# Interleaving the two heads of a pair, token by token, in the query and key buffers of a local attention

## Chip, cores and metric

One Trainium2 chip, one core. The metric is the time of one launch on the device, in microseconds (us), as the median of several runs.

## What is computed

The input x has 2 x 2048 tokens of 256 channels, in f32. First an attention block, then a routed feed-forward block, each with a residual and a normalisation:

```python
qkv = x @ W_attn + b_attn                       # 16 heads of 16 channels
scores = einsum('bhtd,bhsd->bhts', q, k) / 4
scores = where((j <= i) & (j >= i - 64), scores, -inf)
out = softmax(scores) @ v
x = layernorm(x + out @ W_proj + b_proj)
expert_idx = argmax(x @ Wr.T)                   # 8 experts
inter = gelu(x @ W1[expert_idx] + b1[expert_idx])
x = layernorm(layernorm_affine(inter @ Wo + bo + x) + x)
```

## The kernel before, in words

**Order.** The program has a queue for each engine: SP (DMA issues), GpSimd (POOL), ScalarE (ACT), VectorE (DVE) and TensorE (PE), synchronised by semaphores written out by hand. Each runs the loop `for it in range(FIRST, LAST + 1)` over 32 tiles of 128 tokens (`it` from -4 to 31) in software-pipelined order. PE in step `it` does, in this order: `scores(0)`, the output projection of tile it-2, the transposes of x for tile it+4 (line 1641), `scores(1)`, `values(0)`, `scores(2)`, `scores(3)`, `values(1)`, the value projection of tile it+1, the transposes of tile it's maxima (line 1683), the query and key projection of tile it+4 (`queries_keys`, lines 1599 to 1619), and `scores_t(0)` to `scores_t(3)` with the transposes of the attention of tile it-1 between them. Steps -4 to -1 are setup and fill the pipeline. After step 31 the routed feed-forward (`walk_slots`) runs 36 tiles over slots sorted by expert.

**Precision.** Operands in f16 are split into a high and a low part; a product is three matmuls (`product`, line 1428).

**Queries and keys.** `queries_keys` writes 4 groups of 128 output channels (2 for queries, 2 for keys; the index m % 2 is the half: heads 0 to 7 or 8 to 15) for 128 tokens into one PSUM bank, each by 7 matmuls: 2 x 3 of `product` and one for the bias (line 1617). The view of the bank is `ps_qk` (line 259): [query or key, half, token]. ACT copies it to f16 (`qk_hi`, line 955), DVE makes the low part (line 1326). Both wait in the steps' order: ACT after the maxima rows, then come its exps; DVE's low part is the last of its step but for small things. When two tiles are there, SP stores a tile pair to the DRAM tensor `qk_s` by six stores (`store_part`, line 401), then loads it turned, by head: the 16 channels of a head times three terms (high, high, low and their partners) become 48 partitions.

**Loads.** `stacks_begin` (line 476), on SP in even steps, waits for the stores and for the last scores of two pairs before (the buffers `qs` and `ks` are double), and loads the queries (line 483) and the key window of half 0; `stacks_end` (line 487), one step later, loads the window of half 1 and the keys of the second block. A block is 64 queries; its window holds 128 keys and begins 64 tokens earlier, so `windows` (line 467) takes two loads for each half: the new tokens (line 471, runs of 384 bytes) and the last 64 of the pair before (line 474, runs of 128 bytes). PE waits for queries and half 0 at step 0 of a tile's scores, for half 1 (`chunk_ld`) at step 1, for the second block (`second_ld`) at step 2.

**Scores.** They are computed twice. `scores(step)` (line 1560): queries stationary (112 x 64), keys moving (112 x 128), the two heads of a strip side by side in the array's two column halves, 8 matmuls a step, 4 steps a tile. VectorE takes maxima over keys (line 1227). The maxima of all heads are turned by PE (line 1683) into PSUM rows and copied by ScalarE (`maxima_rows`, line 882, two calls a tile, 32 x 1024 elements) into the partitions of `qs` above 96, so that `scores_t(step)` (line 1588: keys stationary, 128 x 128, queries moving, 128 x 64, again 4 x 8) gives scores with the maximum taken off and the mask added; ScalarE's exps (line 879) read them. Mask rows stand in the odd partitions of `ks` (constants), unit rows in those of `qs`; partitions above 96 of `ks` hold window rows that pick a head's maximum. All of these are built at the start by POOL (lines 615 to 693) in a staging area (`mask_w`, `ident_w`, `last_rows`), copied by DVE (line 1013), a DMA (`constant_rows`, line 442), ACT (line 961) and POOL (lines 669, 691).

In memory `qs` is [partition, head, 256 tokens] and `ks` [partition, block, head, 256 tokens], the head index being 2 x pair + half. A matmul's operand takes one head:

```python
def queries(t, c, i, e, b):
    return qs[t // 2 % 2][:, CC * (2 * i + e) + c, t % 2 * P + b * BLK:t % 2 * P + b * BLK + BLK]
def keys(t, c, i, e, b):
    return ks[t // 2 % 2][:, b, CC * (2 * i + e) + c, t % 2 * P:t % 2 * P + P]
```

## Time and profile before

| | us |
|---|---|
| median of 3 runs | 523.68 |
| their range | 520.51 to 526.76 |
| the profiled execution's own time | 522.61 |
| its span, first to last instruction | 520.9 |
| granted TensorE clock over the span | 0.981 of full |

The profile is of one execution. Its times are in us unless marked ns; L1560 is line 1560 of the kernel. PE is TensorE's matmuls, PEld its weight loads, which overlap them; matmuls overlap each other, so that their start distances tell the pace and not their durations. In a row of the timeline stand the start, the time from the first start to the last end, engine, line, operation, output and inputs with shapes, and the count of instructions merged. "[0.75 <-X]" is idle time before it and what ended it; "issue" is idle time in which the profile shows nothing waited for.

### The profile page before, as it was taken

How to read it: one execution, taken by the hardware profiler on the slowest of the kernel's cores; microseconds unless marked ns; L12 is line 12 of the kernel's file. 1: busy time of each engine (PE TensorE's matmuls, PEld its weight loads, DVE VectorE, ACT ScalarE, POOL GpSimd, SP SyncE). 2: the span in 40 equal slices, each digit the busy share in tenths (PEclk: the TensorE clock that was granted, in tenths of full speed). 3: DMA queues.
4: the chain of work that ended last, by engine and by line, in shares of the span. 5: the costliest groups of instructions: out<-in, count | busy, mean ns of one | idle time of the engine just before them, and what ended most of it. 6: DMA issues, size and time to landing. Idle time of an engine off the chain costs nothing. (4 is left out here: it accounts for less than half of the span.)

```text
span 520.9 us, 24517 instructions
## 1 busy us (share of the span) xinstructions
PE 482.8 (93%) x8591; PEld 433.4 (83%) x8591; DVE 423.2 (81%) x1115; ACT 349.6 (67%) x793; POOL 365.3 (70%) x638
## 2 busy tenths in 40 slices
PE   8999998999999989989989899999999999999980
PEld 5678987988988978988877698888999999999970
DVE  6568687789888896877889558799999998998892
ACT  3567585867778785858676686666666666677740
POOL 7983566565757664747566656888888887888884
PEclk9999899999999998989999999999999999999996
DMA  8796486588785777676664122222333366246200
GB/s 225 201 239 168 136 214 170 151 210 215 198 218 167 226 195 191 187 205 182 177 170 99 44 63 64 62 74 74 111 97 84 93 223 243 78 144 222 69 18 14
DMA packets 83000, 77.08 MB, mean 148 GB/s; under 512 B 31046, under 2 KB 74639, under 8 KB 82834
## 3 DMA queue, kind: packets, MB, share of 16 engines
q1 hardware_dynamic: 79250, 66.80, 46.9%
q0 software_dynamic: 3248, 8.41, 4.6%
q8 instruction: 73, 1.20, 1.0%
q14 instruction: 45, 0.37, 0.2%
q10 hardware_dynamic: 384, 0.30, 0.2%
HBM read 43.48 MB, written 23.55 MB: 129 GB/s over the span
## 5 line engine op out<-in xcount | busy, mean ns | idle before, releaser
L1793 PE MATMUL ps<-wo_hi,ks 128*128 128x256 f16 x576 | 128.5, 273 | 5.2 <-DVE ks L1349 5.2
L1811 PE MATMUL ps<-sT_lo,w_hi 128*128 128x128 f16 x496 | 104.3, 219 | 0.0
L1811 PE MATMUL ps<-sT_hi,w_lo 128*128 128x128 f16 x496 | 104.3, 219 | 0.0
L1811 PE MATMUL ps<-sT_hi,w_hi 128*128 128x128 f16 x496 | 104.2, 219 | 0.0
L1227 DVE TENSOR_REDUCE mx<-ps 128x4 bf16<-128x512 f32 x128 | 83.7, 674 | 6.6 <-PE ps L1560 6.3
L736 POOL DMA_INDIRECT slots<-row,slot_of x32 | 33.9, 1059 | 68.3 <-PE ps L1560 39.9
L1793 PE MATMUL ps<-wo_lo,ks 128*128 128x256 f16 x288 | 78.5, 273 | 0.0
L1454 PE MATMUL ps<-v_even,probs 128*64 128x17 f32 x1024 | 68.0, 208 | 2.2 <-issue 1.5
L1454 PE MATMUL ps<-v_odd,probs 128*64 128x17 f32 x1024 | 68.2, 208 | 1.5 <-issue 1.5
L1454 PEld LDWEIGHTS ps<-v_odd,probs 128*64 128x64 f32 x1024 | 64.9, 138 | 3.1 <-issue 3.1
L879 ACT ACTIVATE probs<-ps 128x512 f32<-128x512 f32 x128 | 66.0, 611 | 0.1
L1454 PEld LDWEIGHTS ps<-v_even,probs 128*64 128x64 f32 x1024 | 64.8, 138 | 0.9 <-ACT probs L879 0.8
L885 ACT ACTIVATE qs<-ps 32x1024 f16<-32x1024 bf16 x64 | 61.3, 1004 | 6.0 <-PE ps L1683 5.3
L991 ACT ACTIVATE g_even<-ps,b1T 128x128 f32<-128x128 f32 (+1 forms) x168 | 44.2, 353 | 28.9 <-PE ps L1811 28.5
L1793 PEld LDWEIGHTS ps<-wo_hi,ks 128*128 128x128 f16 x576 | 53.0, 98 | 9.0 <-DVE ks L1349 6.4
L991 ACT ACTIVATE probs<-ps,b1T 128x128 f32<-128x128 f32 x144 | 41.0, 367 | 28.3 <-PE ps L1811 27.7
L941 ACT ACTIVATE v_odd<-ps 128x256 f32<-128x256 f32 x32 | 12.3, 383 | 67.8 <-PE ps L1432 67.8
L1432 PE MATMUL ps<-xT_hi,wa_lo 128*128 128x128 f16 x256 | 52.1, 227 | 0.8 <-issue 0.8
L1432 PE MATMUL ps<-xT_lo,wa_hi 128*128 128x128 f16 x256 | 52.2, 227 | 0.1
L1811 PEld LDWEIGHTS ps<-sT_hi,w_lo 128*128 x496 | 48.5, 98 | 4.4
L1432 PE MATMUL ps<-xT_hi,wa_hi 128*128 128x128 f16 x256 | 52.0, 227 | 0.0
L1588 PE MATMUL ps<-qs,ks 128*128 128x64 f16 x1024 | 48.6, 194 | 3.3 <-DVE attT L1307 1.1
(276 smaller groups left out, 1570.3 us busy)
## 6 DMA issues: line engine op xcount, KB each, us to landing
qk_s<-qk_hi SPq DMA_DIRECT2D x64, 128.0 KB
w_in<-in_L_ffn_W_dram SPq DMA_DIRECT2D x30, 256.0 KB, 2.9
qs<-qk_s SPq DMA_DIRECT2D x16, 384.0 KB, 4.3
ks<-qk_s SPq DMA_DIRECT2D x16, 384.0 KB, 5.4
ks<-qk_s SPq DMA_DIRECT2D x32, 144.0 KB, 4.1
v_odd<-slots SPq DMA_DIRECT2D x32, 128.5 KB
qk_s<-qk_lo SPq DMA_DIRECT2D x30, 128.0 KB
v_odd<-slots SPq DMA_DIRECT2D x30, 128.0 KB
```

The costliest lines, as they stand in the source:

```text
L736: nc.gpsimd.indirect_dma_start(out=slots, out_offset=bass.IndirectOffsetOnAxis(ap=slot_of[n // 2 % 2][:, n % 2:n % 2 + 1], axis=0), in_=ro ...
L879: nc.scalar.activation(probs[:, u, :, :, :], ps_t[step].rearrange("p (i e q) -> p i e q", i=STRIPS, e=2), ACT.Exp, scale=SCALE).then_inc(e ...
L885: nc.scalar.activation(q.rearrange("p (i h) n -> p i h n", i=STRIPS), ps_mx[0:P - ALIGNED].rearrange("p e m n -> p (e m) n").unsqueeze(1) ...
L941: nc.scalar.activation(v_odd[m % VRING][:, :, 0:HD], ps_v[:, 0:C].rearrange("p (h d) -> p h d", d=HD), ACT.Copy)\
L991: last = nc.scalar.activation(g[1 - p][:, ic, n * width:(n + 1) * width], (ps_h_first[half] if j < 0 else ps_h[1 - p][:, half, :])[:, col ...
L1227: nc.vector.tensor_reduce(mx[it % 2][:, at:at + STRIPS], ps_s[step].rearrange("p (i k) -> p i k", k=P), AX.X, ALU.max)\
L1432: last = mm(dst, l, r, start=start and n == 0, stop=stop and n == len(terms) - 1)
L1454: last = mm(ps_num[BLK * b:BLK * b + BLK, head, :], probs[:, 2 * c + b, i, e, :], v[:, head, :], start=True, stop=True, tile_position=(0, ...
L1588: last = mm(ps_t[step][:, at:at + BLK], keys(it, c, i, e, b), queries(it, c, i, e, b), start=i + e == 0 and not first, stop=i + e == STRIP ...
L1793: ins = mm(ps_y[p], h[p][hs][:, ic, :], wo[ws][:, ic, :], start=n == 0, stop=n == 3 * IC - 1)
L1811: up_ins = mm(ps_h[1 - p][:, half, col + m * width:col + (m + 1) * width], weights(ws, owners[m], k, ic), sT[1 - p][ss][:, k, at], start=k ...
```

## The change

The two halves become the innermost index of everything that holds queries and keys. `ps_qk` is read as [query or key, token, half]: a projection matmul writes 128 f32 results at a step of two elements. `qk_hi`, `qk_lo`, `qs`, `ks` and the staging area have the half last; `queries` and `keys` give operands whose elements step by two f16. `qk_s` becomes [query or key, channel, term, token, half] over all tokens, so that the window of a tile pair is one run across the pair boundary: `stacks_begin` issues two loads (queries; the whole key window of both halves), `stacks_end` one (keys of the second block). `chunk_ld` goes. `maxima_rows` issues one instruction for each half, 32 x 512 elements, which writes at a step of two; there are four a tile in place of two. The staging area's mask and unit rows are twice as wide (512 elements), so the memsets and selects that build them are; the copies of them keep their element counts. No other arithmetic changes. The core of the diff:

```diff
-    qk_s = nc.dram_tensor("qk_s", [2, TILES // 2, P, 3, CC, 2 * P], f16, kind="Internal").ap()
+    qk_s = nc.dram_tensor("qk_s", [2, P, 3, N, CC], f16, kind="Internal").ap()
-        qk = [[sb(f"qk{k}_{s}", [P, 2, CC, 2 * P], f16) for s in ("hi", "lo")] for k in range(2)]
+        qk = [[sb(f"qk{k}_{s}", [P, 2, 2 * P, CC], f16) for s in ("hi", "lo")] for k in range(2)]
-        qs = [sb(f"qs{k}", [P, HEADS, 2 * P], f16) for k in range(2)]
-        ks = [sb(f"ks{k}", [P, 2, HEADS, 2 * P], f16) for k in range(2)]
+        qs = [sb(f"qs{k}", [P, PAIRS, 2 * P, CC], f16) for k in range(2)]
+        ks = [sb(f"ks{k}", [P, 2, PAIRS, 2 * P, CC], f16) for k in range(2)]
-        mask_w = stage[:, 0:2 * P]
-        ident_w = stage[:, 2 * P:4 * P]
+        mask_w = stage[:, 0:CC * 2 * P]
+        ident_w = stage[:, CC * 2 * P:CC * 4 * P]
...
         def ps_qk(t):
-            return ps[:, 6 if t < LEAD and t % 2 else 0, :].rearrange("p (w m t) -> p w m t", w=2, m=CC)
+            return ps[:, 6 if t < LEAD and t % 2 else 0, :].rearrange("p (w n m) -> p w n m", w=2, m=CC)
...
-            eng.dma_start(qk_s[w, g, :, term, :, :].rearrange("p m n -> p (m n)"),
-                          qk[g % 2][PARTS[w][term]][:, w, :, :].rearrange("p m n -> p (m n)")).then_inc(qk_st[g % 2], 16)
+            eng.dma_start(qk_s[w, :, term, 2 * P * g:2 * P * (g + 1), :].rearrange("p n m -> p (n m)"),
+                          qk[g % 2][PARTS[w][term]][:, w, :, :].rearrange("p n m -> p (n m)")).then_inc(qk_st[g % 2], 16)
...
-            def windows(g, m, new, landing):
-
-                k = g % 2
-                dst = ks[k][0:ALIGNED:2, 0, :, :].rearrange("r (h m) n -> r h m n", m=CC)[:, :, m, :]
-                sp.dma_start(dst[:, :, BLK:2 * P], new[:, :, m, 0:2 * P - BLK]).then_inc(landing, 16)
-                if g > 0:
-                    prev = qk_s[1, g - 1].rearrange("(h d) j m n -> (d j) h m n", d=HD)
-                    sp.dma_start(dst[:, :, 0:BLK], prev[:, :, m, 2 * P - BLK:2 * P]).then_inc(landing, 16)
+            def stack_rows(w, first, last):
+
+                return qk_s[w, :, :, first:last, :].rearrange("(h d) j n m -> (d j) h (n m)", d=HD)
...
-                windows(g, 0, new, stack_ld[k])
+                sp.dma_start(qs[k][0:ALIGNED:2, :, :, :].rearrange("r h n m -> r h (n m)"),
+                             stack_rows(0, 2 * P * g, 2 * P * (g + 1))).then_inc(stack_ld[k], 16)
+                behind = BLK if g > 0 else 0
+                sp.dma_start(ks[k][0:ALIGNED:2, 0, :, BLK - behind:2 * P, :].rearrange("r h n m -> r h (n m)"),
+                             stack_rows(1, 2 * P * g - behind, 2 * P * (g + 1) - BLK)).then_inc(stack_ld[k], 16)
...
-                windows(g, 1, new, chunk_ld[k])
...
-                    nc.scalar.activation(q.rearrange("p (i h) n -> p i h n", i=STRIPS),
-                                         ps_mx[0:P - ALIGNED].rearrange("p e m n -> p (e m) n").unsqueeze(1)
-                                         .broadcast_to([P - ALIGNED, STRIPS, 2 * CC, BLK]),
-                                         ACT.Copy, scale=1.0 / ONE).then_inc(mxT_out, 1)
+                    for m in range(CC):
+                        last = nc.scalar.activation(
+                            q[:, :, :, m].rearrange("p (i e) n -> p i e n", i=STRIPS),
+                            ps_mx[0:P - ALIGNED, :, m, :].unsqueeze(1).broadcast_to([P - ALIGNED, STRIPS, 2, BLK]),
+                            ACT.Copy, scale=1.0 / ONE)
+                    last.then_inc(mxT_out, 1)
...
             def queries(t, c, i, e, b):
-                return qs[t // 2 % 2][:, CC * (2 * i + e) + c, t % 2 * P + b * BLK:t % 2 * P + b * BLK + BLK]
+                return qs[t // 2 % 2][:, 2 * i + e, t % 2 * P + b * BLK:t % 2 * P + b * BLK + BLK, c]
...
-                return ks[t // 2 % 2][:, b, CC * (2 * i + e) + c, t % 2 * P:t % 2 * P + P]
+                return ks[t // 2 % 2][:, b, 2 * i + e, t % 2 * P:t % 2 * P + P, c]
...
-                        pe.wait_ge(stack_ld[pair % 2], 16 * (pair // 2 + 1 + window_loads(pair)))
+                        pe.wait_ge(stack_ld[pair % 2], 16 * 2 * (pair // 2 + 1))
                         wait(pe, mxT_out, 2 * it)
-                    if step == 1:
-                        pe.wait_ge(chunk_ld[pair % 2], 16 * window_loads(pair))
...
-                        dst = ps_qk(new)[:, m // CC, m % CC, :]
+                        dst = ps_qk(new)[:, m // CC, :, m % CC]
```

## Rows read from the trace of the kernel before

**Rows 1.** The page, part 1: busy us (share of the span) and instructions.

```profile
PE 482.8 (93%) x8591; PEld 433.4 (83%) x8591; DVE 423.2 (81%) x1115; ACT 349.6 (67%) x793; POOL 365.3 (70%) x638
```

**Rows 2.** Stretches, us: PE, PEld, DVE, ACT, POOL busy (count), PEclk, DMA share, GB/s.

```profile
24.00:300.00 276.00, 259.41 (x5561) 230.06 (x5558) 221.94 (x605) 195.68 (x348) 170.84 (x352) 0.98 0.67 180
...
300.00:521.00 221.00, 202.40 (x2852) 189.20 (x2849) 187.11 (x484) 142.26 (x423) 174.22 (x232) 0.98 0.32 102
...
120.00:160.00 40.00, 39.48 (x881) 35.90 (x877) 35.20 (x99) 31.13 (x57) 26.12 (x55) 1.00 0.78 206
```

**Rows 3.** The maxima's transposes (line 1683): all, then two of the timeline.

```profile
L1683 PE MATMUL ps<-ident_b,mx x64: 217/219/314, 28.0 to 295.5; 128*128 128x128 bf16 x64
...
90.18 0.28 PE L1683 MATMUL ps<-ident_b,mx 128*128 128x128 bf16 x2
...
98.04 0.28 PE L1683 MATMUL ps<-ident_b,mx 128*128 128x128 bf16 x2
```

**Rows 4.** Waits: who waited for whom; us in total, times, longest.

```profile
PE ps L1432 <- issue: 3.1, 2, 2.3
...
PE ps L1454 <- issue: 3.0, 2, 1.5
...
PE ps L1560 <- DMA ks<-qk_s: 2.6, 2, 1.7
...
PEld ps L1588 <- ACT qs L885: 4.5, 16, 0.9
```

**Rows 5.** Timeline of PE in a tile, then durations of three lines.

```profile
90.29 0.22 PE L1432 MATMUL ps<-xT_hi,wa_hi 128*128 128x128 f16 x1
...
90.40 0.22 PE L1432 MATMUL ps<-xT_lo,wa_hi 128*128 128x128 f16 x1
...
156.83 0.40 PE L1588 MATMUL ps<-qs,ks 128*128 128x64 f16 x8
...
158.78 0.41 PE L1560 MATMUL ps<-ks,qs 112*64 112x128 f16 x8
...
159.82 0.38 PE L1641 MATMUL ps<-ident,xin 128*128 128x128 f32 x2
...
L1588 PE MATMUL ps<-qs,ks 128*128 128x64 f16 x1024 | 48.6, 194 | 3.3 <-DVE attT L1307 1.1
...
L1560 PE MATMUL ps<-ks,qs 112*64 112x128 f16 x1024 | 46.4, 222 | 3.5 <-DMA ks<-qk_s 2.6 <-DVE mx L1227 0.7
...
L1641 PE MATMUL ps<-ident,xin x46: 272/273/474, 3.0 to 256.0; 128*128 128x128 f32 x46
```

**Rows 6.** Timeline of ScalarE (ACT) in one tile: maxima copies, exps.

```profile
155.46 1.92 ACT L885 ACTIVATE qs<-ps 32x1024 f16<-32x1024 bf16 x2
...
157.90 2.06 ACT L879 ACTIVATE probs<-ps 128x512 f32<-128x512 f32 x4
```

**Rows 7.** Timeline of the setup: POOL, and the first scores of PE.

```profile
1.63 0.51 POOL L619 MEMSET bqk<- 128x512 f16 x1
...
2.20 0.31 POOL L625 MEMSET probs<- 128x256 f16 x1
...
2.66 0.42 POOL L626 TENSOR_SCALAR_AFFINE_SELECT probs<-probs 96x256 f16<-96x256 f16 x1
...
4.15 2.54 POOL L634 TENSOR_SCALAR_AFFINE_SELECT probs<-probs 128x256 f16<-128x256 f16 x2
...
23.33 0.10 POOL L685 MEMSET eps_ffn<- 128x1 f32 x1
...
23.53 0.37 PE L1555 MATMUL ps<-shut,ones_b 1*128 1x512 bf16 x1 [0.75 <-DMA ks<-qk_s]
```

**Rows 8.** DMA: packets of the page, then issues (count, KB, us to landing).

```profile
DMA packets 83000, 77.08 MB, mean 148 GB/s; under 512 B 31046, under 2 KB 74639, under 8 KB 82834
...
ks<-qk_s SPq DMA_DIRECT2D x32, 144.0 KB, 4.1
...
ks<-qk_s SPq DMA_DIRECT2D x30, 48.0 KB, 4.7
```

More of the change, by code:

```diff
@@ L235, in attention_then_routed_ffn @@
         w1_mixed = [[[spare[4 * b + 2 * m + s] for s in range(2)] for m in range(PARTS_M)] for b in range(2)]
[L236 removed]
+        h = [[ks[k][:, :, :, :, :].rearrange("p b h n m -> p (b h n m)")[:, s * IC * P:(s + 1) * IC * P]
               .rearrange("p (i t) -> p i t", i=IC) for s in range(2)] for k in range(2)]
[L238 removed]
+        room = [qs[k][:, :, :, :].rearrange("p h n m -> p (h n m)").bitcast(f32) for k in range(2)]
         xbo, xbe, fin = ([room[k][:, n * C:(n + 1) * C] for k in range(2)] for n in range(3))
@@ L295, in attention_then_routed_ffn @@
         stack_ld = [sem(f"stack_ld{k}") for k in range(2)]
-        chunk_ld = [sem(f"chunk_ld{k}") for k in range(2)]
         second_ld = [sem(f"second_ld{k}") for k in range(2)]
@@ L361, in unit @@
             return step % CC, step // CC, 2 * (step % CC) + step // CC
-        def window_loads(g):
-            return sum(1 + (n > 0) for n in range(g % 2, g + 1, 2))
         def turned(it):
```

68 lines of the change are left out of this document (33 added, 35 removed).

## The prediction

> **What bounds the kernel now.** Read the engines' busy shares first [rows 1]: TensorE (PE) is busy for 93% of the span. The stretches [rows 2] split the span: the change touches what runs to about 300 us (setup and attention); the routed FFN behind it, 221 us, keeps its instructions. In the attention stretch PE is busy for 259.4 of 276 us. The transposes of the maxima come once per tile, the first at 28.0 and the last at 295.5 us [rows 3]: 31 steps, so 8.63 us per tile. The same rows show two of them 7.86 us apart (90.18 and 98.04); seven tiles of 7.86 to 7.90 us stand in this trace. 7.86 us is therefore what PE's own queue needs for a tile, and 0.77 us is the mean of what comes on top. The waits [rows 4] say what that is: 6.1 us in four long gaps put down to "issue", 2.6 us for the stack loads, and the weight load ahead of the second scores waits 4.5 us in 16 tiles for ScalarE's maxima rows. So the loads that the change merges cost PE 2.6 us in this stretch (and 0.75 us ahead of its first scores [rows 7]), while whatever adds PE time adds to nearly every tile.
>
> The spacing of matmuls is read from their starts, not from their durations, since they overlap [rows 5]: projections of 128 columns start at 90.29 and 90.40 with one between them, 55 to 56 ns apart; eight scores of the second kind (64 columns) take 0.40 us with one of 0.19 in it, so 0.21 / 7 = 30 ns apart; eight of the first kind (128 columns, in pairs for the two halves of the array) take 0.41 with 0.22 in it, 27 ns apart or 54 per pair; two transposes of 128 columns in f32 take 0.38 with 0.27 in it, 109 ns apart. TensorE's granted clock is 1.00 in such a stretch [rows 2], its level of 2.4 GHz.
>
> **The change part by part.**
>
> Projection of queries and keys. Per tile 4 x 7 = 28 matmuls now write every second f32 word of their PSUM bank. No row of before has such an output. From below it costs nothing (56 ns apart, as now). From above, take the nearest slower stream of the same 128 columns, the f32 transposes at 109 ns: +53 ns x 28 = 1.48 us per tile. I take the upper end. The reason from rows: 56 ns for 128 columns is 2.3 columns per ns, each 4 bytes on the way out, and no row of [rows 5] writes faster than that per column of the array, so the output side shows nothing to spare; two neighbouring results now lie 8 bytes apart, so if they were written together before, they can't be now. Of the 1.48 us, some 0.2 us fall into what now is waiting (ScalarE's maxima rows, below, end before the longer projection does), leaving 1.28. 28 projections run inside the attention tiles: 28 x 1.28 = 35.8 us. The four of the setup stand on a longer list of waits; I count 2 to 3 us for them.
>
> The Trainium skill bears on this where no row does: "PSUM — Partial Sum Buffer", Specifications, gives 8-byte lines and says that any non-contiguous access pattern slows matmuls significantly. By it the upper end would hold, by the rows alone either could. No run here shows it yet.
>
> Score operands. 32 matmuls of each kind per tile read both operands at a step of two f16. From below nothing; from above, again the f32 row, whose 128 columns bring 4 bytes each past the same port: the first kind 54 to 109 per pair, 16 x 55 = 0.88 us, the second kind 30 to 55, 32 x 25 = 0.80 us, together 1.7 us per tile. I take the lower end: the second kind loads 128 stationary columns within 30 ns [rows 5], 4.3 columns per ns, nearly twice what any moving stream uses, so the reading side shows room that the writing side doesn't.
>
> On this the Trainium skill ("SBUF — State Buffer", in the part on the DMA port swizzle) says that lines are 16 bytes and two hits in one are enough. Four f16 at step two share a line, so by it the scores would keep their pace; no row here tests it.
>
> ScalarE's maxima rows. Two instructions of 1024 elements become four of 512. The two take 1.92 us now, and the four exps, each of 512 elements out of PSUM, take 2.06 [rows 6]: four copies cost about what four exps do, +0.14 us per tile. Behind them on ScalarE wait the high part of queries and keys and the four exps, and behind these VectorE's low part and its maxima. If all of it showed, 32 x 0.14 = 4.5 us; half of the tiles have the weight load waiting there [rows 4], so 2 us. Under the longer projection it is nothing: the copies end 2.06 + 0.3 us after the maxima's transposes, the projection after 28 x 109 ns = 3.05 us.
>
> Setup on GpSimd (POOL). The two memsets and four selects that build the mask and the unit rows double in width. A memset of 256 takes 0.31 us and one of 512 takes 0.51 [rows 7]: +0.2 each. The select of 256 takes 0.42; at twice its width between 0.42 and 0.84. The two selects of the mask take 1.27 us each [rows 7] while VectorE copies the unit rows, and I let them wait for those copies as now. Sum from +0.4 to +3.5 us; I take 2 x 0.2 + 2 x 0.4 = 1.2. It shows: POOL's queue then runs nearly without a gap up to its last constant, ready at 23.43 us, and the first scores start at 23.53 [rows 7]. The window load of the first pair (768 bytes a run in place of 384) ends perhaps 0.6 us later at the same place, so it hides behind that.
>
> Loads. Of each pair six loads become three [rows 8]: 62 window loads of 384 packets (384 or 128 bytes) become 16 of up to 1 KB. PE waits 2.6 + 0.75 us for these in all; I count 1 us gained. Issues on the sync queue cost some 0.6 us each, three fewer per pair, but that queue waits in stretches for the stores and nobody for it. The new addresses put the runs of one load 16 KB apart instead of side by side; a tile pair has over 15 us between load and use, which covers that. Stores move the same bytes in the same runs. The copies of the window rows, the constant rows and the two conversions keep their element counts.
>
> **The sum**, against the profiled execution's own 522.6 us: + 35.8 (projection in tiles) + 2.5 (setup projections) + 1.2 (POOL) + 0 (ScalarE, hidden) - 1 (loads) = + 38.5, so 561.1 us. The median of the runs shown is 1.1 us above the profiled execution: 562 us.
>
> **The rivals.**
>
> A. The strided output costs nothing, the operands neither. For it: no row shows a penalty, and reading has room. Then 1.2 + 2 - 1 = + 2.2 us: 526 us, no difference. It decides at the start distance of the projections: up to about 60 ns apart (28 x 4 ns = 0.1 us per tile) it is this case.
>
> B. The same, and the long "issue" gaps shrink [rows 4]. They are four in 260 us, outside any wait on a semaphore, and if they are the engine's own instructions arriving behind data packets, then fewer packets shorten them: 62 x 384 - 16 x 384 = 17,700 of 83,000 go [rows 8]. It decides where these gaps and the DMA waits together fall under half of their 8.7 us; with all of them gone and ScalarE's copies hidden it is 522.6 + 1.2 - 8.7 = 515.1, in medians 516 us. Against it: the packets removed are the short ones, and most bytes stay. This is the case on the other side: faster.
>
> C. Only the operands cost: 1.7 us per tile, 0.2 in waits, 32 x 1.5 = 48 us, + 1.2: 572 us. For it: the f32 stream at half pace has 4 bytes per column, just what step two spans.
>
> D. Both: 38.5 + 32 x 1.7 = + 93 us: 617 us.
>
> **How the numbers follow.** Forecast (output alone) 0.38, A 0.26, B 0.10, C 0.10, D 0.16. The forecast's own range: the price per matmul from 40 to 65 ns and the setup's share give 550 to 576. The range for 8 in 10 takes in A, most of B and C: 518 to 582; D is left out, and the far end of B. Against no change a measurement of this kernel tells about 1%, here 518.4 to 528.9. Faster: most of B, 0.07. Same: A less its tail and the rest of B, 0.27. Slower: forecast, C, D and A's tail, 0.66.
>
> **What would show it.** In the new profile the projection's starts would stand 100 to 110 ns apart (step right) or still 56 (wrong, then A). The scores would keep 54 per pair and 30; if they stand at 109 and 55, C or D. The shortest distance between two transposes of the maxima would rise from 7.86 to about 9.3 us. ScalarE's four maxima copies would span about 2.06 us. The first scores would start near 24.7 us, or later with the setup's projections. The FFN stretch would keep its 221 us.

## The result and the profile after

The changed kernel takes 564.95 us in the median (564.68 to 566.62, four runs) against 524.78 (520.51 to 526.76) on the same chip: a ratio of 1.078, 95% interval 1.071 to 1.086. The profiled execution took 565.04 us with a span of 563.3; before it was 522.61 with 520.9. The spans differ by 42.4 us.

The page of the new profile, its parts 1 and 3 (busy us and instructions; packets, MB and share of the queues):

```profile
PE 526.2 (93%) x8591; PEld 478.6 (85%) x8591; DVE 427.9 (76%) x1115; ACT 370.2 (66%) x857; POOL 378.9 (67%) x638
...
DMA packets 63832, 77.08 MB, mean 137 GB/s; under 512 B 6502, under 2 KB 55471, under 8 KB 63666
...
q8 instruction: 73, 1.20, 1.0%
```

PE has the same 8591 matmuls and is busy 43.4 us longer [rows 1]; packets fall from 83,000 to 63,832 and those under 512 bytes from 31,046 to 6,502 [rows 8]. So the merged loads move the same 77.08 MB in fewer and larger packets. Then the transposes of the maxima, by instruction and in the timeline, which mark the tiles as in [rows 3]:

```profile
L1676 PE MATMUL ps<-ident_b,mx x64: 218/219/230, 42.9 to 336.3; 128*128 128x128 bf16 x64
```

```profile
100.22 0.28 PE L1676 MATMUL ps<-ident_b,mx 128*128 128x128 bf16 x2
...
109.62 0.28 PE L1676 MATMUL ps<-ident_b,mx 128*128 128x128 bf16 x2
```

The first come at 42.9 us, not 28.0; the last at 336.3, not 295.5; two neighbours are 9.40 us apart where it was 7.86. So the 42.4 us split into setup +14.9, the 31 tile steps +25.9 (9.46 us in the mean, before 8.63), and what follows the last transposes +1.5 (227.0 for 225.4). The window from 342 us on (columns as in [rows 2]) is the routed FFN, as busy as before:

```profile
342.00:564.00 222.00, 202.32 (x2844) 188.65 (x2841) 185.15 (x482) 141.38 (x423) 173.30 (x232) 0.97 0.32 102
```

Now the operations that the prediction argued about. Timeline of PE (start, time, engine, line), then groups of the tile stretch by shape (busy us, mean ns, idle before):

```profile
119.86 0.31 PE L1427 MATMUL ps<-xT_hi,wa_hi 128*128 128x128 f16 x1
...
119.97 0.31 PE L1427 MATMUL ps<-xT_hi,wa_lo 128*128 128x128 f16 x1
```

```profile
L1553 PE MATMUL ps<-ks,qs 112*64 112x128 f16 x992 | 46.3, 224 | 0.3 <-DVE mx L1222 0.3
...
L1581 PE MATMUL ps<-qs,ks 128*128 128x64 f16 x992 | 47.0, 194 | 4.6 <-ACT qs L878 2.6
```

Projections start 0.11 us apart (109 ns over a run of them) where it was 55 to 56. The scores, which now read both operands at a step of two, keep their durations (224 and 194 ns, before 222 and 194 [rows 5]) and nearly their distances: a run of eight takes 205 ns of the first kind and 213 of the second from its first start to its last, before 195 and 204 (medians at full clock, from the traces), so 1.3 to 1.4 ns more for each. The waits of PE in the tile stretch:

```profile
PE ps L1581 <- ACT qs L878: 3.2, 7, 0.9
...
PE ps L1427 <- issue: 0.7, 1, 0.7
...
PE ps L1449 <- issue: 0.5, 1, 0.5
...
PE ps L1507 <- issue: 0.4, 1, 0.4
```

No wait for a stack load is left, and of issue gaps 1.6 us where [rows 4] has 6.1 us in its two lines. The granted clock changed too. Stretches with the columns of [rows 2], the tiles of the kernel before and then of the changed one:

```profile
28.00:296.00 268.00, 252.26 (x5452) 225.13 (x5453) 217.48 (x593) 190.34 (x340) 164.60 (x342) 0.98 0.68 180
```

```profile
43.00:337.00 294.00, 286.95 (x5454) 262.16 (x5454) 217.01 (x593) 210.84 (x401) 163.20 (x339) 1.00 0.58 161
```

The 0.98 is 10.2 us at 0.5 of full (1.2 GHz); the changed kernel has none in its tiles. ScalarE, timeline of a tile and the group, and POOL in the setup:

```profile
119.64 2.48 ACT L878 ACTIVATE qs<-ps 32x512 f16<-32x512 bf16 x4
...
122.39 0.60 ACT L949 ACTIVATE qk_hi<-ps 128x512 f16<-128x512 f32 x1 [0.28 <-PE ps L1610]
```

```profile
L878 ACT ACTIVATE qs<-ps 32x512 f16<-32x512 bf16 x124 | 76.9, 719 | 1.3 <-PE ps L1676 0.5
...
L871 ACT ACTIVATE probs<-ps 128x512 f32<-128x512 f32 x124 | 64.1, 610 | 0.6 <-PE ps L1581 0.3
```

```profile
2.88 2.33 POOL L611 TENSOR_SCALAR_AFFINE_SELECT probs<-probs 96x512 f16<-96x512 f16 x1
...
8.39 6.36 POOL L622 TENSOR_SCALAR_AFFINE_SELECT probs<-probs 128x512 f16<-128x512 f16 x2
...
20.20 4.46 POOL L650 TENSOR_SCALAR_AFFINE_SELECT probs<-probs 32x1024 f16<-32x1024 f16 x1
...
38.23 0.10 POOL L677 MEMSET eps_ffn<- 128x1 f32 x1
```

```profile
38.43 0.37 PE L1548 MATMUL ps<-shut,ones_b 1*128 1x512 bf16 x1 [0.85 <-issue]
```

The four maxima copies take 719 ns each where an exp of as many elements takes 610; they span 2.48 us, before 1.92 for the two [rows 6]. In the setup the select of 512 elements on 96 partitions takes 2.33 us for 0.42 at half the width [rows 7], and the two of the mask 6.36 us together for 2.54. The two for the last rows take 4.46 us each. They have as many elements as before (1024 on 32 partitions), but their pattern now ends in the half, where it ended in 128 tokens; one of them in the kernel before:

```profile
12.03 1.10 POOL L658 TENSOR_SCALAR_AFFINE_SELECT probs<-probs 32x1024 f16<-32x1024 f16 x1
```

POOL's last small memset starts at 38.23 us, and the first scores 0.2 us later, at 38.43, as they did before at 23.33 and 23.53. The whole of the +14.9 us is on that queue: 6.7 in the last rows' selects, 3.8 in the two of the unit rows (2.33 and 2.32 for 0.42 and 0.41), 3.8 in the two of the mask, 0.4 in the two memsets and 0.1 in one other select.

### The profile page after: what moved, and what is told of

Its sections match the earlier page's. It is cut to its first block and busy times, and to the rows that moved or that the text cites. A ratio compares the mean times of both kernels' runs of the same rounds, so it can differ in the third digit from the quotient of the medians.

```text
span 563.3 us, 24504 instructions
## 1 busy us (share of the span) xinstructions
PE 526.2 (93%) x8591; PEld 478.6 (85%) x8591; DVE 427.9 (76%) x1115; ACT 370.2 (66%) x857; POOL 378.9 (67%) x638
## 2 busy tenths in 40 slices
DMA packets 63832, 77.08 MB, mean 137 GB/s; under 512 B 6502, under 2 KB 55471, under 8 KB 63666
## 5 line engine op out<-in xcount | busy, mean ns | idle before, releaser
L1427 PE MATMUL ps<-xT_hi,wa_hi 128*128 128x128 f16 x256 | 80.1, 313 | 8.2 <-DVE xT_lo L1244 7.5
L878 ACT ACTIVATE qs<-ps 32x512 f16<-32x512 bf16 x128 | 79.4, 719 | 4.7 <-PE ps L1676 3.9
L1427 PE MATMUL ps<-xT_hi,wa_lo 128*128 128x128 f16 x256 | 81.5, 318 | 0.0
L1427 PE MATMUL ps<-xT_lo,wa_hi 128*128 128x128 f16 x256 | 81.5, 318 | 0.0
```

The lines of the kernel that those rows point to most:

```text
L878: last = nc.scalar.activation(q[:, :, :, m].rearrange("p (i e) n -> p i e n", i=STRIPS), ps_mx[0:P - ALIGNED, :, m, :].unsqueeze(1).broadc ...
L1427: last = mm(dst, l, r, start=start and n == 0, stop=stop and n == len(terms) - 1)
```

## Experiments

Each was measured against the kernel before on its own chip; ratios are to that, with 95% intervals. The first and last transposes of the maxima, and the shortest distance that recurs in the tiles, are read as above. The table puts them together (us). "Gaps" is the sum of PE's start distances over 0.6 us between first and last transposes, whatever ended them, counted in the trace; "half" is the time there with a granted clock of 0.5, in which PE works at half pace (packed matmuls 107 ns apart for 56, in the last experiment):

| kernel | median | first | last | recurring shortest | gaps | half |
|---|---|---|---|---|---|---|
| before | 524.8 | 28.0 | 295.5 | 7.86 | 15.6 | 10.2 |
| after | 565.0 | 42.9 | 336.3 | 9.40 | 4.8 | 0 |
| after, selects divided | 555.8 | 34.2 | 327.4 | 9.40 | 3.9 | 0 |
| after, output packed | 567.3 | 45.5 | 338.2 | 8.50 | 24.1 | 24.8 |
| both | 559.4 | 35.1 | 330.1 | 8.50 | 27.4 | 25.3 |
| both, copies of maxima packed | 544.4 | 34.9 | 318.7 | 8.03 | 21.4 | 27.3 |
| both, copies as in the old kernel | 543.4 | 33.7 | 314.4 | 7.93 | 23.4 | 17.1 |
| both, old order in DRAM | 553.9 | 35.1 | 325.1 | 8.50 | 22.1 | 20.5 |
| both, copies packed, window later | 543.7 | 34.8 | 319.4 | 8.03 | 23.3 | 23.9 |
| selects divided, copies packed | 556.2 | 34.2 | 330.1 | 9.40 | 4.1 | 3.4 |
| before with strided output | 550.0 | 32.8 | 322.4 | 9.35 | 2.2 | 0 |

The theory at the start: the strided output costs 53 ns a matmul and sets the length of the tiles; the selects with an innermost dimension of two set that of the setup. The rival: the old kernel's gaps and the new load pattern matter as much.

**Selects divided.** The changed kernel; each select with an innermost dimension of 2 becomes two, one per half, at a step of two elements:

```diff
-                link(nc.gpsimd.affine_select(
-                    out=of_blocks(mask_w), in_=of_blocks(mask_w), ...
-                    pattern=[[0, 2], [sign, P], [0, CC]], channel_multiplier=-sign))
+                for m in range(CC):
+                    at = of_blocks(mask_w)[:, :, :, m]
+                    link(nc.gpsimd.affine_select(out=at, in_=at, ...
+                                                 pattern=[[0, 2], [sign, P]], channel_multiplier=-sign))
```

> The changed kernel, but each of GpSimd's selects whose innermost pattern dimension is the half (2 elements, step 0 or -8) is issued once per half, at a step of two, without that dimension. Theory: the short innermost dimension is what makes these selects slow (2.33 us for 512 elements on 96 partitions, 4.46 us for 1024 on 32, against 0.42 us for 256 and 1.10 us for 1024 before), and they delay the whole start. Then each select of one half takes about 0.4 us, the one of last_rows about 0.6, the first transposes of the maxima come near 29 to 31 us instead of 42.9, the tiles keep 9.41 us, and the time falls from 565 by 12 to 14 us, to 551 to 553. Rival 1: a step of two alone is what slows GpSimd; then the selects stay near 2 us for 256 elements each and the time does not fall. Rival 2: the start is late for the new order in DRAM and the wider first window load; then the selects get faster but the first scores stay past 38 us and the time falls by less than 4 us.

Measured 555.78 us (555.53 to 556.42), ratio 1.066 (1.056 to 1.076). Timeline of POOL, and PE's first scores:

```profile
2.87 1.09 POOL L613 TENSOR_SCALAR_AFFINE_SELECT probs<-probs 96x256 f16<-96x256 f16 x2
...
5.92 4.31 POOL L631 TENSOR_SCALAR_AFFINE_SELECT probs<-probs 128x256 f16<-128x256 f16 x4
...
15.51 1.66 POOL L659 TENSOR_SCALAR_AFFINE_SELECT probs<-probs 32x512 f16<-32x512 f16 x2
...
27.95 0.10 POOL L685 MEMSET eps_ffn<- 128x1 f32 x1
```

```profile
29.74 0.38 PE L1556 MATMUL ps<-shut,ones_b 1*128 1x512 bf16 x1
```

The same elements at the same spacing cost less than half in two of the three kinds: two selects of 256 in 1.09 us for one of 512 in 2.33, two of 512 in 1.66 for one of 1024 in 4.46. The mask's gain a third (four of 256 in 4.31 us for two of 512 in 6.36). The last small memset starts 10.3 us earlier, at 27.95. But the scores start at 29.74, 1.8 us behind it: now PE's own setup work ends last, which the timeline shows without idle time from 23.8 us up to them, and 9.2 us of the time come back. Of the rest of POOL's delay (27.95 against 23.33), 1.1 us is in the last rows' selects (1.66 for 1.10, twice) and the others are the memsets and selects of doubled width.

**Output packed.** The changed kernel; the projection writes one half behind the other in PSUM as before, and the interleaving is made by the copies out of it:

```diff
-            return ps[:, ...].rearrange("p (w n m) -> p w n m", w=2, m=CC)
+            return ps[:, ...].rearrange("p (w m n) -> p w m n", w=2, m=CC)
-                        dst = ps_qk(new)[:, m // CC, :, m % CC]
+                        dst = ps_qk(new)[:, m // CC, m % CC, :]
```

ScalarE's high part then writes f16 at a step of two; VectorE's low part is two instructions of 256.

> The changed kernel, but the projection matmuls write their PSUM bank without a step, as in the kernel before; ScalarE's and VectorE's copies out of it write f16 at a step of two instead (one instruction on ScalarE, two of 256 on VectorE instead of one of 512). Loads, buffers, score operands and the slow setup stay. Theory: the step on the output is all that lengthens a tile. Then projection matmuls start 56 ns apart again and not 109, the shortest tile is 7.9 to 8.0 us instead of 9.40, the tiles gain 1.2 to 1.5 us each less what waits come back, and the time falls by 25 to 40 us, to 525 to 540. Rival: the score operands or the two more instructions on ScalarE hold the tile; then the projection's pace returns to 56 ns but the tile stays above 8.6 us and the time falls by under 20 us.

Measured 567.31 us (566.26 to 572.32), ratio 1.091 (1.078 to 1.103): not 25 to 40 us faster than the changed kernel, but no faster at all. Its tiles take 292.7 us where they took 293.4, and its first transposes come 2.6 us later, in a setup whose granted clock is 0.5 from 32.7 to 46.4 us. PE's projections are 56 ns apart again. The transposes and the waits of PE between them:

```profile
63.01 0.28 PE L1676 MATMUL ps<-ident_b,mx 128*128 128x128 bf16 x2
...
71.52 0.28 PE L1676 MATMUL ps<-ident_b,mx 128*128 128x128 bf16 x2
```

```profile
PE ps L1427 <- issue: 9.3, 5, 3.2
...
PE ps L1581 <- ACT qs L878: 6.5, 21, 0.8
...
PE ps L1449 <- issue: 4.5, 3, 1.6
...
PE ps L1553 <- issue: 2.1, 1, 2.1
...
PE ps L1581 <- issue: 1.5, 2, 0.9
```

The recurring shortest tile falls only to 8.50 us, since PE now waits for ScalarE's maxima rows in two tiles of three, and 17.4 us of issue gaps stand where 1.6 stood. On top of that come 24.8 us at half clock where there were none.

**Both.** The two edits above together, nothing else:

> Both of these edits at once: selects per half, and the projection's output without a step. What is left of the change is the merged loads, the score operands at a step of two, the f16 copies written at a step of two and four maxima copies instead of two. If the two causes are all, the time is that of the kernel before with what the loads give: 515 to 527 us. If the long gaps of TensorE that the profile puts down to issue (6.1 us in four before) shrink with 19,000 fewer packets, the attention stretch is 5 us or more shorter than before and the time 515 to 519; if these gaps come back with the shorter tile, 522 to 527. If the score operands or the copies at a step of two cost something that the longer projection hid, 530 or more.

Measured 559.4 us (554.98 to 560.89), ratio 1.072 (1.059 to 1.084), the third branch of what was expected. Waits of PE, then two groups of ScalarE in the tiles:

```profile
PE ps L1457 <- issue: 10.1, 4, 3.9
...
PE ps L1435 <- issue: 9.0, 5, 3.7
...
PE ps L1589 <- ACT qs L886: 7.9, 26, 0.8
```

```profile
L886 ACT ACTIVATE qs<-ps 32x512 f16<-32x512 bf16 x124 | 77.2, 722 | 1.7 <-PE ps L1684 0.9
...
L957 ACT ACTIVATE qk_hi<-ps 128x512 f16<-128x512 f32 x28 | 21.3, 760 | 6.9 <-PE ps L1618 6.4
```

ScalarE's copy of queries and keys takes 760 ns where it writes at a step of two, 597 packed in the changed kernel; the maxima copies 722. The long projection had hidden or kept away three costs: ScalarE's strided writes, the issue gaps and the stretches at half clock (25.3 us here). As the setup is 35.1 us here and not 42.9, the tiles by themselves are as long as in the changed kernel.

**The old kernel with the strided output alone.** All else as before, its small loads too. The copies read the bank at that step, VectorE's in two instructions of 256:

```diff
-            return ps[:, ...].rearrange("p (w m t) -> p w m t", w=2, m=CC)
+            return ps[:, ...].rearrange("p (w t m) -> p w m t", w=2, m=CC)
```

> The kernel before with one edit: the projection matmuls write every second f32 of the bank, and the copies out of it read at that step (VectorE's in two instructions of 256). Loads, buffers and setup as before. Theory: matmuls 109 ns apart, the shortest tile 7.86 + 28 x 0.053 = 9.35 us, and since the tile is longer than what the other engines need, the waits shrink: the attention grows from 267 us (first to last transposes of the maxima) to 290 to 295 us as in the changed kernel, and the time is 545 to 553. Rival: the waits of before (issue gaps, stack loads) were of the DMA traffic and stay, since the traffic is the old one: then the attention grows by the full 28 x 1.48 = 41 us and the time is 562 to 567.

Measured 549.96 us (549.45 to 550.29), ratio 1.055 (1.045 to 1.064). The transposes, and all that PE waits for between them:

```profile
L1683 PE MATMUL ps<-ident_b,mx x64: 218/219/230, 32.8 to 322.4; 128*128 128x128 bf16 x64
```

```profile
PE ps L1683 <- DVE mx L1227: 1.1, 4, 0.4
...
PE ps L1512 <- issue: 0.5, 1, 0.5
...
PE ps L1588 <- ACT qs L885: 0.5, 1, 0.5
```

This one line gives a tile of 9.35 us, 289.6 us of tiles (+22.1). It takes the issue gaps (0.5 us left), the waits for loads and the stretches at half clock away, although 83,000 packets still move. So they vanish because the tile is long, not because the loads were merged. It also delays the first transposes by 4.8 us: the projections of the setup stand on the path there.

**What PSUM output at a step costs by itself.** The old kernel with series of 32 matmuls of 128 columns at PE's start, all on constant data:

```diff
+            def probe(dst, right):
+                for n in range(32):
+                    mm(dst, ones16[:, :], right, start=True, stop=True)
+            probe(bank[:, 0:P], ones16[:, :])
+            probe(bank[:, 0:2 * P].rearrange("p (n m) -> p n m", m=2)[:, :, 0], ones16[:, :])
...
```

> The kernel before with probes on TensorE at its start: series of 32 matmuls of 128 columns, f16 ones, each series with another pattern. In order, twice: output packed, every second f32, every fourth f32, pairs of neighbouring f32 with a gap of two; then once each: moving operand at a step of 2, 4 and 8 f16, output packed. Theory: the output is taken as pairs of neighbouring f32; then at the full clock packed and pairs start 54 to 56 ns apart, every second and every fourth both 107 to 109. Rival 1: any gap slows, then pairs cost as much as every second. Rival 2: cost grows with the distance, then every fourth costs more than every second. For the operand: steps of 2 stay at 56 ns as the scores did; steps of 4 and 8 may be slower, nothing in the traces says.

In the trace, median start distances in ns, in the stretches with a granted clock of 1.00 (2.4 GHz). The very first packed series, at 3 us, starts 106 apart at first, though 1.00 is granted; the 56 is of its repeat at 14.6 us, between other series of 56 and 109:

```
output packed                          56 ns
output every second f32               109
output every fourth f32               109
output pairs of f32 with gaps of two   56
moving operand (f16) at a step of 2, two runs of 64     58
                              of 4, four runs of 32    116
                              of 8, eight runs of 16   227
```

The price is 53 ns a matmul of 128 columns, the same for a step of two and four, and nothing where two neighbouring words are written: what counts is the pair. (Pairs that begin at an odd word were not tried.) The operand results mixed a step with short runs, and were taken again below. The time of this kernel (558.1 us) holds the series and says nothing.

**Maxima copies packed.** From "both"; each copy takes one head of the strip half and both halves, so that it writes f16 side by side and reads PSUM 64 elements apart:

```diff
-                    for m in range(CC):
-                        last = nc.scalar.activation(q[:, :, :, m]..., ps_mx[..., m, :]...
+                    for e in range(2):
+                        last = nc.scalar.activation(
+                            q.rearrange("p (i e) n m -> p e i n m", i=STRIPS)[:, e],
+                            ps_mx[0:P - ALIGNED, e].rearrange("p m n -> p n m").unsqueeze(1)
+                            .broadcast_to([P - ALIGNED, STRIPS, BLK, CC]), ...
```

> The kernel with undivided selects mended and packed projection output (559.4 us, shortest tile 8.50 us), and the copies of the maxima now write packed: two of 512 elements per strip half whose innermost two elements are contiguous in SBUF and read 64 elements apart in PSUM. If it is the write at a step of two on ScalarE that holds the tile at 8.50: each copy back to about 610 ns, shortest tile 8.1 to 8.3 us, 545 to 553 us. If the number of copies or the read costs the same: 719 ns or more a copy, tile 8.50, 556 to 562. If it is the queue of instructions: the gaps of PE put down to issue (21 us) stay in either case.

Measured 544.39 us (541.74 to 549.35), ratio 1.041 (1.028 to 1.054). ScalarE's group and one tile of its timeline, and the transposes:

```profile
L886 ACT ACTIVATE qs<-ps 32x512 f16<-32x512 bf16 x127 | 64.2, 575 | 4.9 <-PE ps L1685 4.0
```

```profile
60.42 2.02 ACT L886 ACTIVATE qs<-ps 32x512 f16<-32x512 bf16 x4
```

```profile
51.79 0.27 PE L1685 MATMUL ps<-ident_b,mx 128*128 128x128 bf16 x2
...
59.81 0.28 PE L1685 MATMUL ps<-ident_b,mx 128*128 128x128 bf16 x2
```

Four copies of 512 elements as in "both", but 575 ns each for 722, 2.02 us together for 2.48. The shortest tile falls from 8.50 to 8.03 us and the time by 15 us. It is the write at a step of two; the count of instructions is worth 0.1 us of the tile at most, as the next kernel shows.

**Copies as in the old kernel.** From "both", two per tile of 1024 elements, packed on both sides; the maxima land with the halves of a head exchanged, which changes values and not the work:

```diff
+                    nc.scalar.activation(q.rearrange("p (i e) n m -> p i e (n m)", i=STRIPS),
+                                         ps_mx[0:P - ALIGNED].rearrange("p e m n -> p e (m n)")...
```

> As the kernel before it in this list, but the copies of the maxima as in the old kernel: two per tile of 1024 elements, packed on both sides; the maxima then land with the two halves of a head in the wrong order, which changes values and no time. If ScalarE's four copies at a step of two are what holds the tile at 8.50 us: both copies together 2.06 us again, shortest tile 7.9 to 8.1, 538 to 546 us with the issue gaps of about 21 us kept. If the tile is held by the other strided write of ScalarE, the copy of queries and keys of 760 ns, or by the operands: tile 8.3 to 8.5, 553 to 560.

Measured 543.37 us (536.74 to 544.63), ratio 1.036 (1.023 to 1.050). The copies take 1004 ns each as before; the recurring shortest tile is 7.93, within 0.07 us of the old kernel's 7.86, with all 64 score matmuls reading at a step of two. This kernel still lacks 20 us in its span (540.9 against 520.9): 5.7 in the setup, 13.2 in the tiles, 1.0 behind. Of the 13.2, the 0.07 us a tile are 2.2 (64 score matmuls at 1.3 ns more each come to 0.08 us a tile); gaps over 0.6 us are 7.8 (23.4 against 15.6). What is left fits the clock: 17.1 us at its half level against 10.2, by an estimate from these numbers (half of that time lost) 3.4 us more.

**Are the gaps made by the new loads?** The order of the stored queries and keys in DRAM as before, the window in two loads:

```diff
-    qk_s = nc.dram_tensor("qk_s", [2, P, 3, N, CC], f16, kind="Internal").ap()
+    qk_s = nc.dram_tensor("qk_s", [2, TILES // 2, P, 3, 2 * P, CC], f16, kind="Internal").ap()
```

> The kernel with both mends (559.4 us, shortest tile 8.50 us, about 21 us of PE gaps put down to issue), with the old order of the stored queries and keys in DRAM (a pair of tiles at a time, contiguous per partition) and the window again in two loads. If the new DRAM order, its bursts or its larger packets are what doubles the issue gaps: gaps back to 6 to 11 us, mean tile 8.8 to 9.0, 543 to 551 us. If they come from the pace of the instruction stream alone: gaps of 18 to 24 us, 556 to 562 us.

Measured 553.87 us (551.91 to 558.61), ratio 1.061 (1.050 to 1.073), with gaps of 22.1 us. By its gaps it is the second branch (18 to 24 us); its time lies between the two. Against "both" (554.98 to 560.89) the runs overlap; the order is worth some 5 us if anything and does not bring the old gaps back.

The other way to make the loads less bursty, from the kernel with packed copies: the window's load moved from `stacks_begin` to `stacks_end`, one tile later:

```diff
             def stacks_begin(g):
...
-                sp.dma_start(ks[k][0:ALIGNED:2, 0, :, BLK - behind:2 * P, :]...
             def stacks_end(g):
...
+                sp.dma_start(ks[k][0:ALIGNED:2, 0, :, BLK - behind:2 * P, :]...
```

> The kernel with both mends and the packed copies of the maxima (544.4 us; gaps of PE over 0.6 us in the attention 21 us, most of them 372 matmuls apart), with the load of the key window issued one tile later, in front of the second key load, so that no stretch has 768 KB of loads issued at once. If the burst of loads delays the transfers of instructions: gaps 10 to 15 us, 534 to 540 us. If only the pace of the instruction stream counts: gaps 18 to 24 us at the same numbers of the matmul stream, 541 to 548 us. If the window lands too late: a wait for ks at the first step of every even tile and a time over 550.

Measured 543.71 us (539.38 to 546.76), ratio 1.031 (1.021 to 1.041), against 544.39 without it: no difference, gaps 23.3 us. The burst is not their cause. One wait for that load appeared, and is among them:

```profile
PE ps L1562 <- DMA ks<-qk_s: 1.9, 1, 1.9
```

**Where the gaps are.** Counting matmuls from the start of the program, gaps recur at the same counts in kernels with the same instructions. All of 1.0 us and more between count 700 and 4700, from the traces (count: length in us):

```
both                   715: 2.2  1087: 4.1  1459: 1.5  1832: 2.7  2699: 1.2  3567: 2.1  3939: 2.5  4311: 3.9
both, copies packed    1459: 3.6  2204: 1.6  2699: 1.2  3567: 2.1  3939: 2.6  4311: 3.7
copies as before       1459: 3.4  1832: 1.9  2204: 1.9  2575: 1.6  3567: 2.5  3939: 2.0  4311: 1.2  4684: 2.5
before                 713: 1.7  1456: 2.6  1939: 1.2  3723: 1.9  4300: 1.7  4671: 1.0
before + 352 matmuls   803: 1.0  3198: 1.5  3941: 2.5  4312: 1.1
```

Those of the kernel before at 1939 and 3723 are its waits for the stack loads, and that of the last line at 803 is a wait for VectorE. Of the rest, most neighbours lie 372 counts or twice that apart. The last line is the first probe, whose 352 extra matmuls shift the same work by 352 counts: the gap at 4300 does not move to 4652, nor those at 713 and 1456 to 1065 and 1808; there are gaps near 3941 and 4312, where the other kernels have them. They belong to the place in the instruction stream, not to the work or to a semaphore.

The place can be told more sharply if every record of PE's queue is counted: matmuls, weight loads and the sequencer's own instructions. In the tiles of all thirteen kernels, probes included, there are 81 gaps of 1.0 us or more. 66 of them stand at a count that is 193 or 194 more than a multiple of 256; of the other 15 the profile puts all but two down to a load or another engine. 372 matmuls are 768 such records, three times 256. One gap in the timeline of "copies as before", and the page's line for the transfers of instructions in its tiles (34 to 314 us):

```profile
217.72 0.21 PE L1455 MATMUL ps<-v_odd,probs 128*64 128x17 f32 x1
...
219.76 0.18 PE L1455 MATMUL ps<-v_even,probs 128*64 128x17 f32 x1 [1.82 <-issue]
```

```profile
q8 instruction: 43, 0.70, 1.2%
```

The q8 packets are 16 KB each (0.70 MB in 43 packets), and there is one for every 256 records of PE: 73 packets for 18,762 records in the changed kernel, 76 for 19,497 in the first probe. In the tiles above they are 6.5 us apart in the mean (280 us / 43). One begins at 217.3 us and takes 1.07, and the gap opens at 217.7 and ends at 219.8. So it is throughout: each of the 66 gaps ends 1.1 to 1.8 us after the end of a q8 packet (1.4 in the median). With packets 6.5 us apart that is no chance: PE waits there for its own instructions, though no run changes these transfers alone. (At other such counts a packet is on its way and PE does not stop, so which packet it needs at a count the trace does not tell.) The Trainium skill ("Advanced Engine Details and Errata", ISA Cache) says that an engine's instruction cache has lines of 16 KB, 256 instructions; the packets and the counts agree with that size. It gives no rule by which only some lines are late, and no run here shows what delays their packets.

The gaps at these counts sum to 7.0 us in the old kernel's tiles, to 17 to 24 us in the six interleaved kernels with the short projection, and to 0 to 3.2 us in the four with the long one. A gap also costs more than itself. All 36 stretches at half clock that begin in the tiles of the thirteen kernels begin 1.3 to 4.2 us after a gap over 0.6 us opened (not every gap is followed by one), and the changed kernel and the old one with strided output have none. The tiles of "both", as a stretch:

```profile
35.00:330.00 295.00, 260.75 (x5444) 228.45 (x5443) 217.61 (x619) 211.79 (x401) 161.69 (x336) 0.96 0.58 159
```

**Is the copies' cost really hidden?** The changed kernel with the diff of "Selects divided" and that of "Maxima copies packed", its output still strided:

> The changed kernel with divided selects (555.8 us, shortest tile 9.40 us, projection output still at a step of two) and the packed copies of the maxima that were worth 15 us where the projection output was packed. If the copies are off the path as long as the projections take 109 ns a matmul: 554 to 557 us, tile 9.35 to 9.40. If the terms add up: shortest tile 8.9, 541 us.

Measured 556.16 us (554.21 to 557.4), ratio 1.056 (1.047 to 1.065), against 555.78 without the packed copies: nothing. ScalarE's copies fall to 576 ns and PE's tile stays 9.40. The same edit is worth 15 us where the projections take 56 ns and zero where they take 109.

**The step of an operand by itself.** Again in front of the old kernel, now with single runs and with packed controls (`wide` holds 1024 ones a partition):

```diff
+            probe(bank[:, 0:P], wide[:, 0:2 * P:2])
+            probe(bank[:, 0:P], wide[:, 0:4 * P:4])
+            probe(bank[:, 0:P], ones16[:, :], left=wide[:, 0:2 * P:2])
...
```

> The old kernel behind series of 32 matmuls of 128 columns, distances at full clock. Moving operand f16 in one run of 128: packed 56 ns, step of two 57, of four 116, of eight 227 if the read of the moving operand is bound by its step (as a first probe with repeated short runs gave); all 56 or 57 if the short runs were what cost there. Packed operand in repeats of 4 x 32 and 8 x 16: 56 in the first case, 110 and more in the second. Stationary operand at a step of two and four: 56 to 60 if weight loads hide behind the matmul as before, 100 or more if the load at a step is slower than the matmul.

Timeline of PE: series at steps of two, four and eight (32 each, merged into one row); then 64 with a packed operand in repeats of 4 x 32 and 8 x 16, and 64 with a stationary operand at steps of two and four:

```profile
7.28 13.55 PE L1532 MATMUL ps<-wide,ones 128*128 128x128 f16 x96
...
40.95 4.58 PE L1532 MATMUL ps<-wide,ones 128*128 128x128 f16 x64
...
45.36 3.73 PE L1532 MATMUL ps<-ones,wide 128*128 128x128 f16 x64
```

By their start distances in the trace, a moving f16 operand at full clock takes 58 ns a matmul at a step of two, 116 at four, 227 at eight (227 also in the part of that series in which the clock is at its half level). Packed it takes 56, in repeats of 4 x 32 and 8 x 16 too (about half of the 4 x 32 ran at the half level, at the 107 ns that packed ones have there). A stationary operand costs nothing at either step: the last row is 64 in 3.73 us with 0.22 in one, 56 apart. So the first probe's prices were those of the step. The time of this kernel (567.7 us, one run) says nothing either.

## Why the prediction was right, and where its terms were not

The total came out at 565.0 for 562 and in the forecast's own case. That it came so close is in part luck: the setup was put 11 us too small (3.7 for 14.9), the tiles 9 too large (34.8 with the loads' gain, for 25.9), and the two errors cancel. The mechanism that decides the case, a strided output at 109 ns, was right.

**Projection output.** Right in mechanism and size. 109 ns apart for 56; the tile grew by 9.40 - 7.86 = 1.54 us for 28 x 53 ns = 1.48. The reason given, that two neighbouring words may be written together, is what the first probe shows: pairs with gaps keep 56 ns, and a step of four costs no more than one of two. The 8-byte line that the Trainium skill gives ("PSUM — Partial Sum Buffer", Specifications) agrees with that; its wording that any non-contiguous pattern slows matmuls does not, since the pairs with gaps are not contiguous and keep 56 ns. The measurement decides.

**Waits absorbed: the term that was mis-sized.** The prediction put 0.2 of the 1.48 us into what was waiting, the ScalarE wait alone. Measured, the mean tile rose by 0.83 us, so 0.71 of 1.54 went into waits: the 0.77 us on top of the shortest tile fell to 0.06. The prediction took 0.77 us as made of gaps and waits alone, and took only 0.2 of it away, ScalarE's part. The issue gaps were read as a fixed cost or as the packets' doing (rival B); they are PE's own instructions arriving late, and a slower stream lets them pass. A third part stood in no term, though [rows 2] shows it as a clock of 0.98: 10.2 us at half clock, some 5 of the 23.9 us (31 x 0.77) by an estimate from these rows, and gone with the gaps. The old kernel with strided output shows it: gaps 2.2 us and no half clock with all the small packets in place. 31 x 0.83 = 25.9 us in place of 35.8.

**Setup on POOL: the other one.** 1.2 us was taken, from a range up to 3.5 (doubling all that it lists gives 3.8); measured +14.9 at POOL's last constant, with 10.3 of it undone by dividing the selects. Two steps failed. One is "at twice its width between 0.42 and 0.84": width was counted, but the new pattern also has an innermost dimension of two elements, and with that a select takes 2.33 us for 512 elements, where two at a step of two take 1.09. The other is that the last rows' selects stood in no term, since their element count stays; their pattern gained the same dimension, and they grew from 1.10 to 4.46 us each, 6.7 us together and the largest part. No row of before had such a shape, and the range didn't reach for it.

**Setup projections.** 2 to 3 us was counted. Alone the strided output delays the first transposes by 4.8 us. In the changed kernel it adds nothing to POOL's +14.9, since POOL's chain ends later than the projections'; with the selects divided the projections' chain ends last, and the scores start 1.8 us behind POOL's last small memset. The chains don't add.

**Score operands.** The lower end was right: 58 for 56 ns at a step of two, 7.93 for 7.86 us a tile. But the rule cited for it does not hold in the probe: a step of four f16 has two hits in each 16 bytes, which the Trainium skill ("SBUF — State Buffer", in the part on the DMA port swizzle) calls enough, and costs 116 ns for 56. The measurement decides: the price begins above two.

**ScalarE.** Hidden, as forecast, and shown to be hidden; its size was wrong. Four copies were put at what four exps take, 2.06 us; they take 2.48, because f16 written at a step of two costs 147 ns more per 512 (722 against 575) elements. With the projection's output packed, this held the tile at 8.50.

**Loads.** The 1 us gained can't be told apart. The waits for loads [rows 4] are gone, but they are gone too in the old kernel with strided output, whose loads were not merged. Rival B's sign came, issue gaps and load waits fell from 8.7 to 1.6 us, but for another reason: they fell as far with all 83,000 packets in place, and with 63,832 and a short tile they stood at 17 us and more. Packets fell by 23% and that was worth nothing that shows.

**Rivals C and D** fall with score distances 1.4 ns longer at most, where they wanted 25 and more; A falls with the 109 ns.

What stays open: why the packets of instructions come late more often in the interleaved kernels with short tiles (gaps at their counts 17 to 24 us) than in the old one (7.0). Neither the order in DRAM nor the burst of loads explains it, and only one execution of each was traced. No version tried beats the old kernel. The closest that leaves nothing out, with divided selects, packed output, packed copies and the window's load moved, is 3.1% behind it (2.1 to 4.1%).

## What to carry to other kernels

Ask of a new layout who pays for the step: an interleaving must be made somewhere, and here PSUM output (double), ScalarE's f16 writes (a quarter more) and POOL's selects over a dimension of two (1.5 to 2.7 times the same elements without it) paid, while the operands, whose step the layout was made of, read it for 1 to 2 ns a matmul. A mend that brings a tile back to its length uncovers what lay below, so try it with the next cover removed as well, and don't add up terms that stand on parallel chains. And look at what an old kernel's idle time is: gaps in which the engine waits for its own instructions, and the half clock behind them, are slack that a slower tile gets for nothing. A select whose element count stays can still change its price when its pattern does.

## What the hardware showed that was not expected

- Matmul output to PSUM in f32: 56 ns for 128 columns packed, 109 at a step of two or four, 56 again for pairs of words with gaps between the pairs.
- A moving f16 operand: 56, 58, 116, 227 ns at steps of one, two, four, eight; a stationary one 56 at steps of one, two and four.
- POOL's affine select with an innermost dimension of two takes 4.4 to 4.6 ns an element (2.33 us for 512, 4.46 for 1024), without it 1.6 to 2.1 at the same spacing (1.09 us for two of 256, 1.66 for two of 512). The mask's, on 128 partitions, take 6.2 ns with it and 4.2 without (6.36 us for two of 512, 4.31 for four of 256).
- ScalarE's copy of 512 elements: 575 ns writing f16 packed and reading PSUM 64 elements apart, 722 writing at a step of two; from f32 in PSUM 597 and 760.
- Gaps of PE of 1 to 4 us outside any semaphore, at some of the multiples of 256 records of its queue, each ending 1.1 to 1.8 us after a 16 KB packet of instructions has landed; at 7.9 us a tile they sum to 7 to 24 us, at 9.4 to 3.2 at most.
- Stretches at half the granted clock, every one of them in the tiles 1.3 to 4.2 us after a gap opened. The old kernel, which has both, ran from 517 to 530 us over all its runs, while the four runs of the changed one stay within 2 us; that this spread comes from the gaps and the clock fits, but only one execution was traced.
